# Ranks of the edge sort in three accumulators in turn, and three columns of eight scattered by GpSimd in place of four

## The chip, the cores and the metric

The kernel runs on one core of one Trainium2 chip. The metric is the device time of one execution in microseconds; the median of the runs counts. Engines are named as in the profile: PE (TensorE's matmuls), PEld (its weight loads), DVE (VectorE), ACT (ScalarE), POOL (GpSimd) and SP (SyncE).

## What is computed

Four graph layers follow each other on 6250 nodes of 256 features and 100000 edges; each ends with a residual sum and a layer norm. The layers gather a row for each edge's source and sum the rows by the edge's target:

```python
edge_index = jnp.stack([src, dst])
x = _layernorm(x + _L0_gnn_ref(x, edge_index, ...))                # conv with batch norms
x = _layernorm(x + _L1_gnn_ref(x, edge_index, edge_type_8, ...))   # 3 relational layers
x = _layernorm(x + _L2_gnn_ref(x, ..., src, dst, edge_type_16))    # messages and a GRU cell
x = _layernorm(x + _L3_gnn_ref(x, edge_index, ...))                # attention
```

The kernel doesn't trust the order of the edges. It first sorts them into buckets of 128 target nodes, padded to chunks of 128 edges (832 chunks). The change is in this sort alone.

## The kernel before

**Edges and groups.** The edges lie as 128 partitions by 784 columns. Eight columns are a group (NG = 8, 98 groups, t counts them), sixteen a block (SB = 16, 49 blocks, NSB; i counts them). The places of the edges of a column are found in four steps.

**Ranks (PE, L1134 to L1141).** For a group PE adds up, in one PSUM accumulator (bank 6, 392 columns: 49 buckets by 8 columns), how many edges of each bucket came before. `tri` counts the partitions ahead within the group, `trest` then adds the rest of the group, so that the accumulator stands at the group's end. Rank t waits on s_read for DVE's reading of group t-1, runs the `trest` matmul of group t-1 (L1139) and the `tri` matmul of group t (L1140), which increments s_rank.

**Slots (DVE, L1612 to L1632).** `rank_of` waits on s_rank, multiplies the ranks with the marks of the buckets (L1616, increments s_read) and reduces them (L1620). Once per block `slots_of` (L1624 to L1632) turns the sums into a chunk number, a partition and a row of the table slots_d, and increments s_slots.

**Placing.** A column of edges is placed in one of two ways. Of each eight columns POOL scatters the first POOL_G = 4 by an indirect DMA into slots_d (L703): column k of a group has a semaphore s_sc[k] of its own, and its scatter waits for the one of the group before on the same semaphore. The other four are routed by PE: DVE makes two one-hot marks of the column, over partitions (`ohp`, L1641) and over chunks (`ohc`, L1642); ACT scales the first by the two payload words (`lhs`, L774, two copies); PE multiplies them (L1149 into columns 0 to 511, L1151 into the other 320) and adds up in banks 0 to 3 over the whole sort. Marks and copies lie in a ring of ROUTES = 6; s_sort, incremented by each route, frees a place for DVE and ACT.

**Order.** DVE works two blocks ahead with ranks and slots (AHEAD_SB = 2): in each half of block i it makes the marks of the half and then reads the rank of the same half of block i+2. PE's program has the same order: rank, the routes of the half, rank, the routes of the other half, and then `gram(i)` (L1157, four matmuls on X, bank 7). All queues are in order. Before its first route PE sums X's rows in bank 5 (L1164), which ACT reads at L764 and L765, and ACT's copies of the routes stand behind these two. After the sort SP waits for all scatters and loads slots_d (L575), and DVE adds the routed words (L1681).

Of the kernel before, what the change touches and what calls it, by code (L numbers as in the profile page):

```python
# [22 lines left out]
ACT = mybir.ActivationFunctionType  # L23
# [3 lines left out]
N, D, E = 6250, 256, 100000  # L27
NT = -(-N // P)
# [5 lines left out]
NG = 8  # L34
NSB = -(-(EC + 1) // SB)
EP = NSB * SB
TB = EP // NG
POOL_G = (4, 4)
ROUTES = 6
AHEAD_SB = 2  # L40
TU = 7
TI = NT // TU
U = 16
# [35 lines left out]
READY0 = 4  # L79
assert 0 < ETAIL <= 32 and EC % NG >= max(POOL_G) and EC // NG == TB - 1  # L80
assert max(N, P << LOW_BITS) <= 30 * 1024 and LEAST % (1 << LOW_BITS) == 0
assert NT == TU * TI and NCH == U * CI and U == 2 * GR and NCH % GR == 0
assert all(U * min(t + READY, CI) * NT >= (t + 1) * NCH for t in range(NT)) and CI - READY <= NT
# [41 lines left out]
def program(nc, a, out):  # L125
    ctx = ExitStack()
    with ctx:
        def sb(name, shape, dt=F32):
            return ctx.enter_context(nc.sbuf_tensor(name, shape, dt))

        def sem(name):
            return ctx.enter_context(nc.semaphore(name))

        def dram(name, shape, dt=F32):
# [12 lines left out]
        X = sb("X", [P, NT, D])  # L147
# [7 lines left out]
        g = sb("g", [P, U, D + R2])  # L155
# [7 lines left out]
        ones = sb("ones", [P, P])  # L163
# [5 lines left out]
        ps = ctx.enter_context(nc.psum_tensor("ps", [P, 8, 512], F32))  # L169
# [3 lines left out]
        mine = AY[:, 0:m_words].bitcast(F16).rearrange("p (b e) -> p b e", e=EP)  # L173
# [13 lines left out]
        tri, trest, ones_h, col_h = (Y[:, y0 + k * (P // 2):y0 + (k + 1) * (P // 2)].bitcast(F16) for k in range(4))  # L187
# [20 lines left out]
        marked = gflat[:, 3 * EP:3 * EP + 2 * NG * NT].rearrange("p (s g b) -> p s g b", s=2, g=NG)  # L208
        base_b = gflat[:, 3 * EP + 2 * NG * NT:3 * EP + 3 * NG * NT]
# [98 lines left out]
        assert o3 <= NT * D  # L308
        own = [Y[:, scratch3 + b * TU * D:scratch3 + (b + 1) * TU * D] if b < TI - 2 else
               gflat[:, (b - TI + 2) * TU * D:(b - TI + 3) * TU * D] for b in range(TI)]  # L310
        own = [v.rearrange("p (t d) -> p t d", d=D) for v in own]
        assert scratch3 + (TI - 2) * TU * D <= NT * D

# [18 lines left out]
        def lhs(r, k):  # L332
            return spare[r // 2][:, r % 2, k, :]

        product_t = Y[:, y_prod:y_prod + KD * D].rearrange("p (k d) -> p k d", k=KD)
        b2_row, mu_row, cov, nmu_row = rows0[:, 2, :], rows0[:, 3, :], rows0[:, 4:6, :], rows0[0:1, 6, :]
# [15 lines left out]
        s_prep_act = sem("s_prep_act")  # L352
# [9 lines left out]
        s_wt = sem("s_wt")  # L362
        s_mine = sem("s_mine")
        s_rank = sem("s_rank")
        s_read = sem("s_read")
# [6 lines left out]
        s_blank_d = sem("s_blank_d")  # L372
        s_sc = [sem(f"s_sc{k}") for k in range(max(POOL_G))]
        s_loaded = sem("s_loaded")
# [111 lines left out]

        sort_cols = [NG * s + k for s in range(2) for k in range(POOL_G[s], NG)]
        per_sb, half_sb = len(sort_cols), (0, NG - POOL_G[0], len(sort_cols))
        out_uses = [(NT + 1) // 2, NT // 2]
# [8 lines left out]
        def bucket_by_size(engine, t):  # L498

            _, values = nc.values_load_multi_w_load_instructions(  # L500
                order_of[0:1, bass.ds(t, 1)], engines=(engine,), min_val=0, max_val=NT - 1,
                skip_runtime_bounds_check_because="the buckets' numbers in another order")
            return values[0]
# [28 lines left out]
        def batch(v, b):  # L532
            return v[:, TU * b:TU * (b + 1), :]

# [15 lines left out]
        def _(sp):  # L550
# [20 lines left out]

            for k in range(max(POOL_G)):
                sp.wait_ge(s_sc[k], 16 * NSB * sum(k < n for n in POOL_G))
            sp.wait_ge(s_read, TB)
# [168 lines left out]
        def _(act):  # L743
# [17 lines left out]
                     ps[:, k, :].rearrange("p (b k o) -> p k b o", b=KD, k=KD)).then_inc(s_wt, 1)  # L761

            act.wait_ge(s_prep_pe, PREP_PE["csum"])
            act.activation(mu_row, ps[:, 5, 0:D], ACT.Copy, scale=1.0 / N).then_inc(s_prep_act, 1)  # L764
            act.activation(nmu_row, ps[0:1, 5, 0:D], ACT.Copy, scale=-1.0).then_inc(s_prep_act, 1)  # L765

            for i in range(0, NSB):
                for q in range(per_sb):
                    at, n = sort_cols[q], per_sb * i + q
# [3 lines left out]
                    for k in range(WORDS):  # L773
                        ins = act.activation(lhs(r, k), ohp[:, r, :], ACT.Copy,  # L774
                                             scale=payload[:, bass.ds(SB * i + at, 1), k])
# [303 lines left out]
        def _(pe):  # L1079
# [7 lines left out]
            for w in range(4):  # L1087
                for b in range(KD):
                    for k in range(KD):
                        at = (b * KD + k) * P  # L1090
                        ins = pe.transpose(ps[:, w, at:at + P], nat0[:, w, b, k * P:(k + 1) * P], ident[:, :])
# [27 lines left out]
            def marks(t):  # L1119
                return mine[:, :, NG * t:NG * (t + 1)]  # L1120

            def over_groups(v):
                return v.rearrange("p (b g) -> p b g", g=NG)

            ranks = over_groups(ps[:, 6, 0:NT * NG])

            pe.wait_ge(s_const, 7)
            pe.wait_ge(s_mine, NT)
            for t in range(TB):
                ins = pe.matmul(over_groups(ps[:, 7, 0:NT * NG]), ones_h, marks(t), start=(t == 0), stop=(t == TB - 1))  # L1130
            ins.then_inc(s_prep_pe, 1)
            pe.wait_ge(s_prep_dve, PREP_DVE["base"])
            pe.matmul(ps[:, 6, 0:NT * NG], ones[0:1, :], base_b[0:1, :], start=True, stop=False, skip_group_check=True)

            def rank(t):

                if t:
                    pe.wait_ge(s_read, t)
                    pe.matmul(ranks, trest, marks(t - 1), start=False, stop=False, skip_group_check=True)  # L1139
                pe.matmul(ranks, tri, marks(t), start=False, stop=(t == TB - 1), skip_group_check=True)\  # L1140
                    .then_inc(s_rank, 1)  # L1141

            def route(n):

                r, last = n % ROUTES, n == per_sb * NSB - 1
                pe.wait_ge(s_ohc, n + 1)
                pe.wait_ge(s_lhs, ROUTES + n + 1)
                for k in range(WORDS):
                    pe.matmul(ps[:, 2 * k, :], lhs(r, k), ohc[:, r, 0:512], start=(n == 0), stop=last,  # L1149
                              skip_group_check=True)  # L1150
                    ins = pe.matmul(ps[:, 2 * k + 1, 0:NCH - 512], lhs(r, k), ohc[:, r, 512:NCH], start=(n == 0),  # L1151
                                    stop=last, skip_group_check=True)
                ins.then_inc(s_sort, 1)

            def gram(t):
                for k in range(KD):
                    pe.matmul(ps[:, 7, k * D:(k + 1) * D], X[:, t, k * P:(k + 1) * P], X[:, t, :],  # L1157
                              start=False, stop=False, skip_group_check=True)

            for t in range(2 * AHEAD_SB):  # L1160
                rank(t)
            pe.wait_ge(s_x_in, 32)
            for t in range(NT):
                ins = pe.matmul(ps[:, 5, 0:D], ones[:, :], X[:, t, :], start=(t == 0), stop=(t == NT - 1))  # L1164
            ins.then_inc(s_prep_pe, 1)
            pe.matmul(ps[:, 7, :], zrow[:, 0:P], zrow, start=True, stop=False, skip_group_check=True)
            pe.wait_ge(s_prep_act, PREP_ACT["nmu"])
            for i in range(NSB):
                for q in range(per_sb):
                    if i + AHEAD_SB < NSB and q in half_sb:  # L1170
                        rank(2 * (i + AHEAD_SB) + half_sb.index(q))
                    route(per_sb * i + q)
                gram(i)
            for k in range(KD):
                ins = pe.matmul(ps[:, 7, k * D:(k + 1) * D], nmu_row[:, k * P:(k + 1) * P], mu_row[0:1, :], start=False,
                                stop=True, skip_group_check=True)
# [8 lines left out]
            for o, lo, hi in ((ps[0:1, 6, :], 0, 512), (ps[0:1, 7, 0:NCH - 512], 512, NCH)):  # L1185
                pe.matmul(o, ones[0:NT, 0:1], count_m[:, 1, lo:hi], start=True, stop=False)
                ins = pe.matmul(o, minus_one[0:NT, :], count_m[:, 2, lo:hi], start=False, stop=True)
# [345 lines left out]
        def _(dve):  # L1533
# [74 lines left out]
                link(dve.tensor_tensor(bases[:, :, k + 1], bases[:, :, k], counts[:, :, k], ALU.add))  # L1608
            dve.sem_inc(s_prep_dve, 1)

            ranked = ps[:, 6, 0:NT * NG].rearrange("p (b g) -> p b g", g=NG)

            def rank_of(t, at, s):

                dve.wait_ge(s_rank, t + 1)
                ins = dve.tensor_tensor(marked[:, s].rearrange("p g b -> p b g"), ranked, mine[:, :, bass.ds(at, NG)],  # L1616
                                        ALU.mult)
                ins.then_inc(s_read, 1)
                dve.wait_ge(s_read, t + 1)
                link(dve.tensor_reduce(slot_f[:, NG * s:NG * (s + 1)], marked[:, s], AX, ALU.add))  # L1620
# [23 lines left out]

            for i in range(-AHEAD_SB, NSB):
                for s in range(2):
                    if i >= 0:
                        dve.wait_ge(s_slots, i + 1)
                        for q in range(half_sb[s], half_sb[s + 1]):
                            slot_marks(i, q)  # L1650
                    if i + AHEAD_SB < NSB:
                        rank_of(2 * (i + AHEAD_SB) + s, SB * (i + AHEAD_SB) + NG * s, s)
                if i + AHEAD_SB < NSB:
# [15 lines left out]
            for k in range(2):  # L1669
                ins = dve.tensor_scalar(count_m[:, 1 + k, :], count_m[:, 0, :], bound_c[:, k:k + 1], prow[0:NT, :],  # L1670
                                        ALU.is_ge, ALU.mult)
# [149 lines left out]
            for k in range(KD):  # L1821
                ins = dve.tensor_scalar(diagonals[:, KD + k, :], ident[:, :], cvec[:, k:k + 1], None, ALU.mult)
# [379 lines left out]
```

## Time and profile before

| what | us |
|---|---|
| median of 3 runs | 8975.67 (8972.37 to 9003.58) |
| the profiled execution | 8997.92 |
| its span, first to last instruction | 8996.0 |
| PE busy in the span | 6359.2 (71%) |
| POOL busy | 5138.8 (57%) |
| DVE busy | 4786.9 (53%) |
| ACT busy | 2385.3 (27%) |
| mean granted TensorE clock | 0.832 of full speed |

The profile is of one execution. Busy shares are means over stages of very different kind; the sort takes less than the first tenth of the span, all that follows gathers and sums rows. An idle time is put down to a releaser, "remote" and "another core or an unknown queue" being those for which the profile finds none. The ends of matmuls are modelled, their starts are measured.

### The profile page before, as it was taken

The page shows a single profiled execution, that of the slowest core. Times are in us where ns is not written, and L with a number is a line of the kernel's source. Part 1 is how long each engine was busy: PE and PEld are TensorE (multiplying, and loading weights), DVE is VectorE, ACT ScalarE, POOL GpSimd, SP SyncE. Part 2 cuts the span into 40 slices and gives each one's busy share as a digit, 9 for nine tenths or more (in the row PEclk, how much of TensorE's full clock was granted, in tenths as well). Part 3 has the DMA queues.
Part 4 walks back from the last instruction along what each step waited for, and adds up shares of the span by engine and source line. Part 5 has one row for each costly group of instructions (what it writes and reads, how often), then busy time and mean ns, then how long its engine had stood idle before and what let it go on. Part 6 is the DMA issues. An engine that isn't in the chain of part 4 may idle for free.

```text
span 8996.0 us, 103600 instructions
## 1 busy us (share of the span) xinstructions
PE 6359.2 (71%) x25277; PEld 4099.7 (46%) x25277; DVE 4786.9 (53%) x16507; ACT 2385.3 (27%) x7342; POOL 5138.8 (57%) x5401
## 2 busy tenths in 40 slices
PE   6665777779777777677776555555777776888881
PEld 3333555554345545444444334333444444656551
DVE  5555455545444444344343444444555556888788
ACT  2331111112111111011111222220222224666665
POOL 3555666650266666566665666665666655655550
PEclk8887787879888899788888776667998887999995
DMA  1002333333444445444445666664333335666662
GB/s 50 2 2 58 113 90 90 90 80 131 139 128 135 134 135 132 110 135 136 137 136 148 210 212 208 213 199 105 90 92 91 89 79 161 191 190 190 188 184 72
DMA packets 562307, 1141.83 MB, mean 127 GB/s; under 512 B 115031, under 2 KB 307516, under 8 KB 561598
## 3 DMA queue, kind: packets, MB, share of 16 engines
q0 software_dynamic: 252160, 659.72, 27.8%
q1 hardware_dynamic: 195886, 366.27, 11.7%
q10 hardware_dynamic: 113680, 109.21, 3.6%
q8 instruction: 228, 3.74, 0.2%
q14 instruction: 353, 2.89, 0.1%
HBM read 822.31 MB, written 312.46 MB: 126 GB/s over the span
## 4 chain that ended last, share of the span: by engine, by line
PE 40%; another core or an unknown queue 21%; DVE 15%; issue 15%; ACT 4%; DMA 1%; DVEq 1%; ACTq 1%; POOL 0%; SPq 0%; POOLq 0%
PE ps L1108 12%; PE ps L1324 6%; PE ps L1294 4%; DVE AY L1775 4%; PE ps L1512 3%; PE ps L1499 2%; PE ps L1490 1%; PE ps L1485 1%; PE ps L1456 1%; DVE oh L1758 1%; DVE rows L1758 1%; PE ps L1097 1%; DVE AY L2061 1%; PE ps L1457 1%
## 5 line engine op out<-in xcount | busy, mean ns | idle before, releaser
L1775 DVE TENSOR_TENSOR AY<-AY,ps 128x256 f32 (+1 forms) x4160 | 1735.6, 417 | 3183.6 <-remote 1671.9
L718 POOL DMA_INDIRECT g<-rel_d,edges x2496 | 2365.3, 948 | 1716.6 <-issue 667.7
L1108 PE MATMUL ps<-g,rows 128*128 128x256 f32 (+1 forms) x4160 | 1375.1, 453 | 282.5 <-DVE AY L1775 121.4
L1108 PE MATMUL ps<-g,oh 128*128 128x256 f32 (+1 forms) x4160 | 1381.6, 450 | 146.1 <-DVE oh L1758 54.7
L1108 PEld LDWEIGHTS ps<-g,rows 128*128 128x128 f32 x4160 | 866.4, 228 | 648.8 <-issue 396.8
L718 POOL DMA_INDIRECT g<-rows_d,edges x832 | 800.9, 963 | 504.2 <-issue 206.7
L1108 PEld LDWEIGHTS ps<-g,oh 128*128 128x128 f32 x4160 | 868.0, 227 | 406.8 <-issue 212.9
L718 POOL DMA_INDIRECT g<-in_x,edges x832 | 793.8, 954 | 448.8 <-issue 211.2
L1324 PE MATMUL ps<-AY,turned 128*128 128x512 f32 x1568 | 829.1, 656 | 202.7 <-ACT turned L745 114.6
L2048 DVE TENSOR_REDUCE AY<-ps 128x4 f32<-128x512 f32 x832 | 570.0, 685 | 202.8 <-PE ps L1490 128.3
L1758 DVE TENSOR_SCALAR oh<-col,edges 128x128 f32<-128x128 f32 x2080 | 617.0, 297 | 48.5 <-DMA marks_d<-oh 24.1
L1758 DVE TENSOR_SCALAR rows<-col,edges 128x128 f32<-128x128 f32 x2080 | 607.3, 292 | 51.3 <-issue 41.4
L745 ACT ACTIVATE wt<-ps 128x512 f32<-128x512 f32 (+1 forms) x448 | 250.0, 558 | 1410.6 <-remote 595.8
L703 POOL DMA_INDIRECT slots_d<-AY,g x392 | 381.1, 972 | 362.4 <-DVE g L1632 245.6
L738 POOL DMA_INDIRECT g<-att_d,edges x416 | 394.1, 947 | 330.3 <-PE ps L1512 174.4
L738 POOL DMA_INDIRECT AY<-att_d,edges x416 | 393.9, 947 | 272.1 <-PE ps L1512 175.5
L1324 PEld LDWEIGHTS ps<-AY,turned 128*128 128x128 f32 x1568 | 324.4, 211 | 468.2 <-issue 318.5
L745 ACT ACTIVATE turned<-ps 128x256 f32<-128x256 f32 (+1 forms) x343 | 141.4, 412 | 1150.7 <-remote 920.2
L745 ACT ACTIVATE AY<-ps 128x512 f32<-128x512 f32 (+3 forms) x421 | 179.1, 443 | 999.9 <-remote 674.2
L1023 ACT ACTIVATE g<-g 128x64 f32<-128x64 f32 x1664 | 419.2, 334 | 0.0
L1023 ACT ACTIVATE AY<-AY 128x64 f32<-128x64 f32 x1664 | 418.7, 334 | 0.0
L1097 PE MATMUL ps<-AY,turned 128*128 128x256 f32 x784 | 235.4, 427 | 199.5 <-DVE AY L1890 93.4
(378 smaller groups left out, 9566.2 us busy)
## 6 DMA issues: line engine op xcount, KB each, us to landing
rel_d<-wt ACTq DMA_DIRECT2D x392, 256.0 KB
turned_d<-AY SPq DMA_DIRECT2D x104, 512.0 KB
wt<-turned_d SPq DMA_DIRECT2D x104, 512.0 KB
AY<-marks_d SPq DMA_DIRECT2D x104, 512.0 KB
rel_d<-g SPq DMA_DIRECT2D x49, 1024.0 KB
g<-rel_d,edges POOLq DMA_INDIRECT x2496
marks_d<-oh SPq DMA_DIRECT2D x104, 256.0 KB
marks_d<-rows SPq DMA_DIRECT2D x104, 256.0 KB
```

The lines of the kernel that those rows point to most:

```text
L703: pool.indirect_dma_start(out=slots_d, out_offset=bass.IndirectOffsetOnAxis(ap=slot_row[:, at:at + 1], axis=0), in_=payload[:, at, :], in_ ...
L718: pool.indirect_dma_start(out=g[:, j, 0:width], out_offset=None, in_=table, in_offset=bass.IndirectOffsetOnAxis(ap=edges[:, word, c:c + 1] ...
L738: pool.indirect_dma_start(out=group_at(k)[:, j, 0:W4], out_offset=None, in_=att_d, in_offset=bass.IndirectOffsetOnAxis(ap=edges[:, 0, c:c ...
L745: return act.activation(o, v, ACT.Copy)
L1023: ins = act.activation(row[:, h * F:(h + 1) * F], row[:, h * F:(h + 1) * F], ACT.Copy, scale=row[:, D + h:D + h + 1])
L1097: ins = pe.matmul(o, turned[:, b, k * P:(k + 1) * P], w[:, k, :], start=(k == 0), stop=(k == KD - 1))
L1108: ins = pe.matmul(sum_slot(order, j), one_hot_at(j % OHS), g[:, j, 0:width], start=True, stop=True)
L1294: ins = pe.matmul(ps[:, q, :], turned[:, b, k * P:(k + 1) * P], relations[0][:, k, q * 512:(q + 1) * 512], start=(k == 0), stop=(k == KD - 1))
L1324: ins = pe.matmul(ps[:, 4 + q % 2, :], turned[:, 0, k * P:(k + 1) * P], w[:, k, q * 512:(q + 1) * 512], start=(k == 0), stop=(k == KD - 1))
L1758: dve.tensor_scalar(one_hot_at(j % OHS), col[:, :], edges_f[:, 2, k:k + 1], None, ALU.is_equal)\
L1775: dve.tensor_tensor(tile_at(A, t, width), tile_at(A, t, width), sum_slot(order, j), ALU.add)\
L2048: dve.tensor_reduce(red[:, c % 4, :], ps[:, SP_BANKS[c % len(SP_BANKS)], :].rearrange("p (h e) -> p h e", h=H), AX, ALU.max)\
```

## The change

Three things change. POOL scatters three columns of eight, with three semaphores, and PE routes the other five; a block has 10 routes in place of 8. The ranks are kept in three accumulators (banks 4, 5 and 6) in turn: group t uses bank 4 + t % 3, waits for DVE's reading of group t-3, adds the rest of group t-3, the whole of the groups t-2 and t-1 (`ones_h`), and its own `tri`. And PE issues ranks two groups further ahead (RANKS_ON = 2). The sum over X moves from bank 5 to bank 0, behind a wait for ACT's copies of the weights.

```diff
-POOL_G = (4, 4)
+POOL_G = (3,3)
 ROUTES = 6
 AHEAD_SB = 2
+RANKS, RANK_BANK, RANKS_ON = 3, 4, 2
...
-            act.activation(mu_row, ps[:, 5, 0:D], ACT.Copy, scale=1.0 / N).then_inc(s_prep_act, 1)
-            act.activation(nmu_row, ps[0:1, 5, 0:D], ACT.Copy, scale=-1.0).then_inc(s_prep_act, 1)
+            act.activation(mu_row, ps[:, 0, 0:D], ACT.Copy, scale=1.0 / N).then_inc(s_prep_act, 1)
+            act.activation(nmu_row, ps[0:1, 0, 0:D], ACT.Copy, scale=-1.0).then_inc(s_prep_act, 1)
...
-            ranks = over_groups(ps[:, 6, 0:NT * NG])
+            def ranks(t):
+                return over_groups(ps[:, RANK_BANK + t % RANKS, 0:NT * NG])
...
-            pe.matmul(ps[:, 6, 0:NT * NG], ones[0:1, :], base_b[0:1, :], start=True, stop=False, skip_group_check=True)
+            for t in range(RANKS):
+                pe.matmul(ps[:, RANK_BANK + t, 0:NT * NG], ones[0:1, :], base_b[0:1, :], start=True, stop=False,
+                          skip_group_check=True)
 
             def rank(t):
 
-                if t:
-                    pe.wait_ge(s_read, t)
-                    pe.matmul(ranks, trest, marks(t - 1), start=False, stop=False, skip_group_check=True)
-                pe.matmul(ranks, tri, marks(t), start=False, stop=(t == TB - 1), skip_group_check=True)\
+                if t >= RANKS:
+                    pe.wait_ge(s_read, t - RANKS + 1)
+                    pe.matmul(ranks(t), trest, marks(t - RANKS), start=False, stop=False, skip_group_check=True)
+                for u in range(max(t - RANKS + 1, 0), t):
+                    pe.matmul(ranks(t), ones_h, marks(u), start=False, stop=False, skip_group_check=True)
+                pe.matmul(ranks(t), tri, marks(t), start=False, stop=(t >= TB - RANKS), skip_group_check=True)\
                     .then_inc(s_rank, 1)
...
-            for t in range(2 * AHEAD_SB):
+            for t in range(2 * AHEAD_SB + RANKS_ON):
                 rank(t)
+            pe.wait_ge(s_wt, 4)
             pe.wait_ge(s_x_in, 32)
             for t in range(NT):
-                ins = pe.matmul(ps[:, 5, 0:D], ones[:, :], X[:, t, :], start=(t == 0), stop=(t == NT - 1))
+                ins = pe.matmul(ps[:, 0, 0:D], ones[:, :], X[:, t, :], start=(t == 0), stop=(t == NT - 1))
...
-                    if i + AHEAD_SB < NSB and q in half_sb:
-                        rank(2 * (i + AHEAD_SB) + half_sb.index(q))
+                    if q in half_sb and 2 * (i + AHEAD_SB) + half_sb.index(q) + RANKS_ON < TB:
+                        rank(2 * (i + AHEAD_SB) + half_sb.index(q) + RANKS_ON)
                     route(per_sb * i + q)
...
-            ranked = ps[:, 6, 0:NT * NG].rearrange("p (b g) -> p b g", g=NG)
+            def ranked(t):
+                return ps[:, RANK_BANK + t % RANKS, 0:NT * NG].rearrange("p (b g) -> p b g", g=NG)
...
-                ins = dve.tensor_tensor(marked[:, s].rearrange("p g b -> p b g"), ranked, mine[:, :, bass.ds(at, NG)],
+                ins = dve.tensor_tensor(marked[:, s].rearrange("p g b -> p b g"), ranked(t), mine[:, :, bass.ds(at, NG)],
                                         ALU.mult)
```

## Rows read from the trace of the kernel before

**Rows 1.** The page, section 5: costliest groups of the whole span.

```profile
L1775 DVE TENSOR_TENSOR AY<-AY,ps 128x256 f32 (+1 forms) x4160 | 1735.6, 417 | 3183.6 <-remote 1671.9
```

**Rows 2.** Windows: stage, its length, busy us and instructions by engine, clock, DMA.

```profile
91.00:748.00 657.00, 415.76 (x1925) 210.36 (x1924) 380.67 (x1236) 239.96 (x772) 366.18 (x377) 0.82 0.02 2
...
775.00:8996.00 8221.00, 5877.28 (x23088) 3848.79 (x23088) 4341.43 (x15125) 2131.03 (x6549) 4747.38 (x4992) 0.83 0.47 137
```

**Rows 3.** The chain of waits, 91 to 748 us: start, length, what.

```profile
by line: another core or an unknown queue 31.2%; issue 14.7%; DVE edges L1642 10.8%; PE ps L1149 8.2%; DVE g L1616 8.0%; DVE edges L1641 7.7%; PE ps L1151 5.7%; DVE g L1620 5.0%; ACT oh L774 1.8%; PE ps L1157 1.5%; ACT turned L774 1.2%; ACT
...
319.00 12.13 another core or an unknown queue
...
502.10 7.04 another core or an unknown queue
```

**Rows 4.** Table of waits in the sort: us in total, times, longest.

```profile
DVE g L1616 <- remote: 201.8, 34, 12.7
...
DVE edges L1641 <- remote: 23.7, 6, 7.2
```

**Rows 5.** Timeline around a wait of DVE: start, length, engine, line, [idle before].

```profile
307.90 0.17 DVE L1632 SCALAR_TENSOR_TENSOR g<-g 128x16 int32<-128x16 f32 x1
...
316.30 0.18 DVE L1632 SCALAR_TENSOR_TENSOR g<-g 128x16 int32<-128x16 f32 x1
...
316.50 0.33 PE L1139 MATMUL ps<-AY 128*128 128x392 f16 x1
316.67 0.33 PE L1140 MATMUL ps<-AY 128*128 128x392 f16 x1
...
320.21 0.30 PE L1151 MATMUL ps<-edges,oh 128*128 128x320 f16 x1
...
331.16 0.82 DVE L1616 TENSOR_TENSOR g<-ps,AY 128x392 f32<-128x392 f32 x1 [12.16 <-remote]
...
332.03 0.51 PE L1139 MATMUL ps<-AY 128*128 128x392 f16 x1 [11.53 <-DVE g L1616]
```

**Rows 6.** Timeline of POOL: firsts of two runs of scatters, the last before a pause.

```profile
308.35 1.09 POOL L703 DMA_INDIRECT slots_d<-AY,g  x1 [1.80 <-DVE g L1632]
...
327.43 0.96 POOL L703 DMA_INDIRECT slots_d<-AY,g  x1 [0.30 <-issue]
...
499.54 1.08 POOL L703 DMA_INDIRECT slots_d<-AY,g  x1 [1.32 <-issue]
```

**Rows 7.** The table slots_d: scatters and the load back, durations, first and last start.

```profile
L703 POOL DMA_INDIRECT slots_d<-AY,g x392: 952/958/1179, 64.2 to 746.5; - x196
...
L575 SPq DMA_DIRECT2D AY<-slots_d x1: 352/352/352, 748.7 to 748.7; - x1
```

**Rows 8.** Timeline of DVE without waits: marks, ranks and slots.

```profile
332.61 0.26 DVE L1641 TENSOR_SCALAR edges<-AY,g 128x128 f16<-128x128 f16 x1
...
333.12 0.25 DVE L1641 TENSOR_SCALAR edges<-AY,g 128x128 f16<-128x128 f16 x1
...
334.64 0.81 DVE L1616 TENSOR_TENSOR g<-ps,AY 128x392 f32<-128x392 f32 x1
...
336.09 0.17 DVE L1624 CAST g<-g 128x16 int32<-128x16 f32 x1
...
336.90 0.25 DVE L1641 TENSOR_SCALAR edges<-AY,g 128x128 f16<-128x128 f16 x1
```

**Rows 9.** Timeline of PE: gram, two routing matmuls in a dense stretch, one after a gap.

```profile
305.63 1.03 PE L1157 MATMUL ps<-X 128*128 128x256 f32 x4
...
310.54 0.38 PE L1149 MATMUL ps<-edges,rows 128*128 128x512 f16 x1
...
310.89 0.38 PE L1149 MATMUL ps<-edges,rows 128*128 128x512 f16 x1
...
755.33 0.64 PE L1149 MATMUL ps<-edges,turned 128*128 128x512 f16 x1
```

**Rows 10.** Groups of instructions by line, 91 to 748 us: the scatters.

```profile
L703 POOL DMA_INDIRECT slots_d<-AY,g x376 | 365.6, 972 | 297.5 <-DVE g L1632 185.3 <-issue 112.2
```

## The prediction

> **What bounds the kernel now.** I read the windows by stage first: the change touches only the sort, and [rows 2] show that its routed part runs from 91 to 748 us, 657 us for 49 blocks of 16 columns, 13.4 us each. The reader is to see that no engine is full there: PE is busy 416 us, DVE 381, Pool 366, ACT 240, the DMA engines 2%. The costliest line of the page [rows 1] belongs to the graph layers that follow, 8221 us which the edit doesn't touch, so whatever the sort gains or loses passes to the end: the first gather waits for the sorted edges.
>
> Then I read the chain of waits of the same stretch [rows 3]. 31.2% of it, 205 us, lies at no engine but at "an unknown queue", in a few long pieces (12.1 us at 319.0, 7.0 us at 502.1). The table of waits says whose they are [rows 4]: DVE sat 201.8 us before L1616, the reading of the ranks, 34 times, longest 12.7. The timeline takes one apart [rows 5]: PE ran the second rank matmul L1140 at 316.67, DVE ended its last mark at 319.0, PE its last routing matmul at 320.5. Then PE, ACT and DVE stand still until L1616 starts at 331.16. That instruction waits for one thing, the increment of s_rank that L1140 carries, 14 us old by then. PE's next rank matmul starts at 332.03, as soon as the read has ended. So the increment was late, not the work.
>
> What was active meanwhile is Pool. It scatters 16 columns on end from 308.35 to 328.4, one per 1.26 us [rows 5, 6], and DVE comes free 2.8 us after that. The onset fits as well. After a pause of Pool of 1.80 us (308.35) the stall starts 10.7 us into the scatters, in the second block of the run; the first block went through in 8.4 us (DVE's L1632 at 307.90 and 316.30 [rows 5]). After a pause of 1.32 us (499.54 [rows 6]) it starts at 502.1, only 2.6 us in. I read this so: while Pool issues scatters without a break, semaphore increments of PE come late, and a pause of about two microseconds clears them. Now a block costs Pool 8 x 1.26 = 10.1 us and DVE only some 8.3, so Pool never pauses until the stall itself makes it. That is a reading of coincidences, and the forecast hangs on it.
>
> **The change, part by part.**
>
> Pool scatters 3 of 8 columns. 6 x 1.26 = 7.6 us per block in place of 10.1 [rows 6]. With three semaphores in place of four a scatter now waits for the one three before it, issued 3.8 us earlier. The last scatter is issued at 746.5 and SP, which waits for all of them to land, issues the reading back at 748.7 [rows 7]: landing takes at most 2.2 us, so this costs nothing. If it took the 5.05 us that four scatters last, the upper bound that the pitch leaves, Pool would be back at 10.1.
>
> DVE makes 10 pairs of marks in place of 8. A pair takes 0.51 us (332.61 to 333.12), a rank 1.45 (334.64 to 336.09, multiply and reduce), the slots 0.81 (336.09 to 336.90) [rows 8]. Before: 8 x 0.51 + 2 x 1.45 + 0.81 = 7.8, measured 8.4 in the block without a stall, so 0.6 for collisions. After: 8.8, with the same collisions 9.4 us.
>
> PE routes 10 in place of 8: each four matmuls, two pitches of 0.35 (310.54 to 310.89), so 7.0 us. Its ranks take four matmuls per group, not two (one more matmul for each of the two groups between): 8 per block, which follow each other at 0.17 (316.50, 316.67 [rows 5]), 1.4 us. The four matmuls of L1157 take 1.03. Together 9.4 us at 2.4 GHz, against 7.3 before [rows 9]. PE and DVE are then level and both above Pool's 7.6.
>
> ACT makes 20 scaled copies at 0.32 (an estimate from 240 us busy over 49 x 16 copies, 0.31 each [rows 2]): 6.3 us, under both.
>
> Ranks two groups ahead in three accumulators. In place of the group that DVE reads next, PE has issued two more by then: a late s_rank increment may be late by a block before DVE notices. At the same time PE's wait on s_read is for a read three groups back. Behind rank's wait stand all routing matmuls of the half block, and ACT and DVE wait for those through the ring of six; with the wait gone early this costs nothing. The bank moved to 0 for the column sum waits for four copies that ACT did long before 60 us, nothing. Two accumulators more to start: two short matmuls, under 2 us, hidden before 91 us, where all wait for X's sums.
>
> So a block takes 9.4 us at best. At that pace Pool works 7.6 and pauses 1.8 us or more, the pause after which [rows 6] show a whole block without a stall, and if it is too short, the stall lengthens it. To the 9.4 I add 0.6 us for two engines that are both nearly full and hand over through six slots. 10.0 us per block: 49 x (13.4 - 10.0) = 167 us less.
>
> Bounds: below, DVE without collisions, 8.8 us, -225 us. Above, every wait stays, and the added DVE work comes on top, +49 x 1.0.
>
> One rule speaks against the change. The row: 376 scatters took 365.6 us, 0.97 each, beside 0.96 of an undisturbed one in the timeline [rows 6, 10], so DVE's marks cost Pool about 0.01 us per scatter. The Trainium skill (SBUF — State Buffer, the shared port pair) says that a VectorE tensor_scalar in a two-port mode blocks GpSimd from writing descriptors for its whole length. By the row Pool needs 7.6 us; by the rule up to 7.6 plus the marks' length. The trace doesn't bear it out at that size.
>
> **Rivals.**
> - Ring of six. Late increments are those of the routes (s_sort) too, and DVE and ACT wait for a route six back, only about half a block. For: DVE already waits 23.7 us at L1641 for an unknown releaser [rows 4]. Against: in a block after a pause it doesn't. If half the 205 us stays: 10.0 + 2.1 = 12.1 us per block, -64 us, 8912.
> - No change in sum: the stalls keep their length because another block's worth of work meets them. 13.4 per block, 8976.
> - The other side: the lateness follows PE's own traffic of matmuls and increments, not Pool's scatters. Before the stall PE had been running its matmuls densely and at the short duration of 2.4 GHz, which speaks for it; that they end 2.8 us after Pool's last scatter speaks against it. Then the 205 us stay and each block pays DVE's extra 1.0: +50 us, 9026. It decides if stalls are seen with Pool idle.
> - Clock. A routing matmul of 512 columns takes 0.64 us after a gap of PE, 0.38 in a dense stretch [rows 9]; all at 1.2 GHz a block's 9.4 us double to 18.8, +265 us, 9241. Against it: PE would be nearly always busy. The Trainium skill (TensorE: Matmul & The Clock Gate, Part 1) says the throttled state is the default and activity releases it; the trace agrees, the mean granted clock being 0.82 in the routed part.
> - Pool locked out, the rule above worked out from rows: 10 x (0.25 + 0.43) = 6.8 us of marks [rows 8] on top of 7.6 makes 14.4 us per block, +49 us, 9025.
>
> **How the numbers follow.** The sum is made against the profiled execution, 8997.92 us with a span of 8996.0: 8831. It is 22 us above the median 8975.67, so I forecast 8809. Chances: forecast (9.4 to 11.5 us per block, 8780 to 8883) 0.70; ring of six 0.12; no change 0.07; PE's own traffic 0.07; clock 0.03; Pool locked out 0.01. Faster by over 0.5% (45 us, about what this kernel's runs can tell from no change) 0.82, same 0.07, slower 0.11. The likeliest's own range is 8780 to 8883; reaching down for less than full collisions and up over the ring of six gives 8765 to 8935, which leaves out some 0.18.
>
> **What would show it.** Right: the routed part is 490 us long; Pool scatters in runs of 6 with a pause of 2 us or more; DVE's wait before L1616's successor falls from 202 us to under 20; granted clock above 0.95 there; everything after the sort keeps its length. Wrong: long waits on "an unknown queue" that moved to the marks or to ACT's copies (ring of six); waits that start with Pool idle (PE's traffic); a granted clock near 0.5; scatters longer than 1.1 us. What would break the sum is above all that the link between Pool's unbroken scatters and the late increments is only a coincidence.

## The result, and the profile after

The changed kernel takes 8766.01 us (median of 4 runs, 8756.10 to 8773.54), the kernel before 8979.73 beside it: ratio 0.976, 95% interval 0.9743 to 0.9776. That is 214 us less. The direction and what bound the kernel were forecast; the size was not: 167 us and a range down to 8765 were forecast, and the ratio puts the changed kernel at 8760 on the scale of the median shown before, just under the range.

The routed part of the sort by windows (stage, length, busy us and instructions of PE, PEld, DVE, ACT, POOL, then the granted clock, the DMA share and GB/s):

```profile
91.00:539.00 448.00, 445.62 (x2471) 246.98 (x2470) 433.20 (x1418) 294.78 (x956) 277.22 (x284) 1.00 0.03 3
```

It ends at 539 us where it ended at 748 [rows 2]. DVE is busy 97% of it and PE by its modelled ends 99%; the clock is granted in full, 0.82 before. The table of waits of this stretch, longest first:

```profile
POOL slots_d L704 <- DVE g L1640: 106.7, 47, 14.7
POOL slots_d L704 <- issue: 72.6, 233, 1.8
ACT turned L775 <- DVE edges L1649: 50.9, 32, 2.1
ACT oh L775 <- DVE edges L1649: 49.6, 31, 2.0
ACT rows L775 <- DVE edges L1649: 47.8, 30, 2.1
PEld ps L1155 <- issue: 32.1, 123, 0.3
DVE edges L1649 <- PE ps L1157: 19.2, 2, 16.8
```

The wait of 201.8 us before the reading of the ranks (L1616 in [rows 4], now L1624) has no row any more. ACT waits for DVE's marks and Pool for its slots, 47 times, 2 us each but for the start. The chain of waits has "an unknown queue" no longer among its first twelve parts, where it was 31.2% [rows 3]:

```profile
by line: DVE edges L1650 31.9%; DVE edges L1649 19.5%; DVE g L1624 15.1%; DVE g L1628 11.6%; issue 8.7%; PE ps L1155 2.4%; DVE g L1632 1.8%; DVE g L1633 1.8%; PE ps L1157 1.8%; DVE g L1636 1.4%; DVE g L1638 0.9%; DVE g L1634 0.8%; DVEq L164
```

The timeline of Pool and DVE through one block (start, length, [idle before]), beside [rows 5, 6 and 8]:

```profile
304.50 0.17 DVE L1640 SCALAR_TENSOR_TENSOR g<-g 128x16 int32<-128x16 f32 x1
...
304.96 1.09 POOL L704 DMA_INDIRECT slots_d<-AY,g  x1 [1.98 <-DVE g L1640]
...
305.13 0.25 DVE L1649 TENSOR_SCALAR edges<-AY,g 128x128 f16<-128x128 f16 x1
...
305.64 0.40 DVE L1649 TENSOR_SCALAR edges<-AY,g 128x128 f16<-128x128 f16 x1
...
306.85 0.64 DVE L1650 TENSOR_SCALAR edges<-edges,g 128x832 f16<-128x832 f16 x1
...
307.41 0.81 DVE L1624 TENSOR_TENSOR g<-ps,AY 128x392 f32<-128x392 f32 x1
...
311.40 0.96 POOL L704 DMA_INDIRECT slots_d<-AY,g  x1 [0.31 <-issue]
...
313.88 0.17 DVE L1640 SCALAR_TENSOR_TENSOR g<-g 128x16 int32<-128x16 f32 x1
...
314.33 1.09 POOL L704 DMA_INDIRECT slots_d<-AY,g  x1 [1.97 <-DVE g L1640]
```

Slots at 304.50 and at 313.88: a block takes 9.38 us, again and again. Pool scatters six columns in 7.4 us and pauses 1.97. A mark takes 0.25 us; the one at 305.64, begun 0.7 us after the start of a scatter, takes 0.40. The first gather of the layers, which is what the rest waits for, starts 206 us earlier (774.37 in the trace before):

```profile
568.48 0.99 POOL L719 DMA_INDIRECT g<-in_x,edges  x1 [24.19 <-DVE edges L1694]
```

From there to the end it is 8201 us against 8222. In nine other runs whose layers are the same this rest took 8182 to 8216, so I take these 20 us for spread of the layers and not for the sort; no run shows it, and 8222 is the longest of all.

### The profile page after: what moved, and what is told of

Its sections match the earlier page's. It is cut to its first block, busy times and chain, and to the rows that moved or that the text cites. A ratio compares the mean times of both kernels' runs of the same rounds, so it can differ in the third digit from the quotient of the medians.

```text
span 8769.9 us, 105363 instructions
## 1 busy us (share of the span) xinstructions
PE 6380.8 (73%) x25864; PEld 4099.8 (47%) x25864; DVE 4844.9 (55%) x16703; ACT 2445.7 (28%) x7538; POOL 5049.1 (58%) x5303
## 4 chain that ended last, share of the span: by engine, by line
PE 40%; another core or an unknown queue 21%; DVE 16%; issue 14%; ACT 4%; DMA 1%; DVEq 1%; ACTq 1%; SPq 0%; POOL 0%; POOLq 0%
PE ps L1109 11%; PE ps L1331 6%; PE ps L1301 4%; PE ps L1519 4%; DVE AY L1783 3%; PE ps L1463 2%; PE ps L1506 2%; DVE edges L1650 2%; PE ps L1497 2%; PE ps L1492 2%; PE ps L1464 1%; PE ps L1098 1%; DVE AY L2069 1%; DVE edges L1649 1%
## 5 line engine op out<-in xcount | busy, mean ns | idle before, releaser
L1783 DVE TENSOR_TENSOR AY<-AY,ps 128x256 f32 (+1 forms) x4160 | 1744.1, 419 | 3173.0 <-remote 1681.1
L1109 PE MATMUL ps<-g,rows 128*128 128x256 f32 (+1 forms) x4160 | 1327.6, 440 | 278.7 <-DVE AY L1783 113.0
L1109 PEld LDWEIGHTS ps<-g,rows 128*128 128x128 f32 x4160 | 835.4, 220 | 636.0 <-issue 381.6
L704 POOL DMA_INDIRECT slots_d<-AY,g x294 | 287.9, 979 | 246.2 <-DVE g L1640 169.3
```

The source lines that it names most:

```text
L1109: ins = pe.matmul(sum_slot(order, j), one_hot_at(j % OHS), g[:, j, 0:width], start=True, stop=True)
L1783: dve.tensor_tensor(tile_at(A, t, width), tile_at(A, t, width), sum_slot(order, j), ALU.add)\
```

## The experiments

**Each half of the change alone.** The first kernel is the changed one with `POOL_G = (4, 4)`: only the accumulators and the ranks ahead are left. The second is the kernel before with three of eight scattered.

```diff
-POOL_G = (3,3)
+POOL_G = (4, 4)
```

> The changed kernel with four of eight columns scattered again, so that only the three accumulators and the ranks issued ahead are left of the change. If unbroken scatters of Pool delay the increments (my theory), Pool needs 10.1 us per block and never pauses by itself, the waits move from the ranks to the ring of six (marks L1649, copies L775), and a block takes 11.5 to 13.4 us: 0 to -95 us against before. If the ranks ahead are what removed the stalls (rival), a block takes Pool's 10.1 us: -160 us or more.

Measured: ratio to before 1.0003 (0.9992 to 1.0014). No gain at all. The waits have moved, as a view of waits in the sort shows:

```profile
DVE edges L1649 <- remote: 198.9, 40, 8.4
```

and the timeline of a stall (start, length, [idle before]):

```profile
301.78 0.17 DVE L1640 SCALAR_TENSOR_TENSOR g<-g 128x16 int32<-128x16 f32 x1
...
308.16 0.25 DVE L1649 TENSOR_SCALAR edges<-AY,g 128x128 f16<-128x128 f16 x1 [4.22 <-remote]
...
312.97 0.96 POOL L704 DMA_INDIRECT slots_d<-AY,g  x1 [0.30 <-issue]
...
315.22 0.26 DVE L1649 TENSOR_SCALAR edges<-AY,g 128x128 f16<-128x128 f16 x1 [5.14 <-remote]
...
320.31 0.17 DVE L1640 SCALAR_TENSOR_TENSOR g<-g 128x16 int32<-128x16 f32 x1
```

The ranks are there in time; now it is the marks that wait for an old route's s_sort. 201.8 us before L1616 became 198.9 before L1649. Making one consumer deaf to late increments handed the wait to the next.

> The kernel before with three of eight columns scattered and nothing else: ranks in one accumulator, each waiting for the reading before. My theory: Pool works 7.6 us per block and pauses, so the 12 us stalls are gone; late increments in the last third of a run of scatters can cost the second rank of a block a microsecond or so; 9.4 to 11 us per block, -120 to -200 us. Rival (the ranks ahead removed the stalls): the stalls stay, and DVE's two extra pairs come on top, 13.4 to 14.4 us per block, 0 to +50 us.

```diff
-POOL_G = (4, 4)
+POOL_G = (3, 3)
```

Measured: 8766.10 us, ratio 0.9749 (0.9726 to 0.9771). The whole gain, with the ranks in one accumulator. The wait before the ranks, 201.8 us before, in its table of waits:

```profile
DVE g L1616 <- remote: 1.8, 1, 1.8
```

**Is it Pool's scatters, and is it their being unbroken?** Two edits of the kernel before, both with four of eight columns. In the first Pool does something else than scatter after each eighth scatter:

```diff
 ROUTES = 6
+PAUSES = 6
...
                         in_=payload[:, at, :], in_offset=None).then_inc(s_sc[k], 16)
+                if t % 2:
+                    for _ in range(PAUSES):
+                        paused += 1
+                        pool.memset(gflat[:, 4016:4352], 0.0).then_inc(s_pause, 1)
+                        pool.wait_ge(s_pause, paused)
```

> The kernel before, four of eight scattered, with six small chained memsets of Pool after every eighth scatter: Pool gets some 2.5 us more work per block in which it scatters nothing. My theory: the long waits before L1616 (202 us) nearly vanish, and a block takes what Pool now needs, 12.1 to 12.8 us: -30 to -65 us, although Pool has more to do. Rival, the lateness follows PE's own traffic or Pool's being busy with anything: the waits stay and the time is the same or higher, up to +120 us.

Measured: 8926.03 us, ratio 0.9934 (0.9915 to 0.9953), some 56 us faster with more to do for the very engine that was the suspect. Pool's timeline and DVE's row in the table of waits:

```profile
314.29 0.96 POOL L706 DMA_INDIRECT slots_d<-AY,g  x1 [0.31 <-issue]
315.25 3.10 POOL L712 MEMSET g<- 128x336 f32 x6
318.62 0.96 POOL L706 DMA_INDIRECT slots_d<-AY,g  x1 [0.28 <-POOL g L712]
```

```profile
DVE g L1624 <- remote: 52.1, 22, 3.4
```

The six memsets take 3.1 us together, a block therefore 13 us of Pool, and Pool is busy without a gap: 475 of 612 us by the windows, and what is left is the 0.30 us between its instructions. Yet DVE's wait falls from 201.8 to 52.1 us and the longest from 12.7 to 3.4. So it isn't Pool's being busy that holds the increments up, it is scattering without a break.

> The kernel before without any scatter (left out: the columns that Pool places, so half the edges are missing from the output; every other engine does the same work). My theory: no wait for an unknown releaser before L1616, blocks of 8.3 us, DVE's own work, the routed part 410 us: -240 to -260 us. Rival, PE's own traffic of matmuls and increments: the 12 us waits stay, and the time is within 20 us of before.

```diff
             for k in range(max(POOL_G)):
-                sp.wait_ge(s_sc[k], 16 * NSB * sum(k < n for n in POOL_G))
+                pass
...
-                for k in range(POOL_G[t % 2]):
+                for k in range(0):
```

Measured: 8693.71 us, ratio 0.967 (0.9649 to 0.969), 288 us less. Two slots rows of its timeline, and its window:

```profile
306.50 0.18 DVE L1632 SCALAR_TENSOR_TENSOR g<-g 128x16 int32<-128x16 f32 x1
...
314.30 0.17 DVE L1632 SCALAR_TENSOR_TENSOR g<-g 128x16 int32<-128x16 f32 x1
```

```profile
91.00:453.00 362.00, 346.94 (x1861) 189.78 (x1859) 352.13 (x1206) 227.75 (x746) 0.00 (x0) 1.00 0.00 1
```

7.8 us per block and no wait for the unknown. PE sends its increments more densely than in the kernel before, and none is late: PE's own traffic is out as a cause. And 7.8 is exactly the sum of DVE's instructions in [rows 8], so the 0.6 us of collisions that I added belongs to the scatters, not to DVE.

**Late increment or held-up DVE?** The views name the releaser of these waits "remote", and by them alone DVE itself could have been held up. The kept traces also record single increments with their times, though not all of them (81 of the 98 of s_rank in the kernel before), and these show that DVE starts as soon as the increment is recorded. The increment of [rows 5], from the matmul of 316.67, is recorded at 331.13, 0.03 us before L1616 starts. Four of s_sort stand behind it, at 331.19, 331.25, 331.31 and 331.37, for routes that PE had ended by 320.5. Over the routed part the recorded increments of s_rank come up to 14.3 us after the end of their matmul, while those that DVE and ACT make come within 0.02 us. In e4 those of s_rank do so too.

In the changed kernel PE's increments are late still, s_rank's by up to 3.5 us: one comes at 304.12, 1.1 us after a run's last scatter has ended, and five of s_sort follow it in 0.3 us. But DVE reads that rank at 311.73, and nobody waits. In e2 s_rank's come up to 2.8 us late, which cost the 1.8 us above.

**How long a run, or how much load?** The kernel of e2 with the same work per block, in runs of twelve:

```diff
-                if t % 2 == 0:
-                    pool.wait_ge(s_slots, t // 2 + 1)
+                if t % 4 == 0:
+                    pool.wait_ge(s_slots, min(t // 2 + 2, NSB))
```

> As e2_pool_only (three of eight scattered, one accumulator), but Pool waits for the slots of two blocks and then scatters both: the same work per block, 7.6 us, in runs of 12 scatters (15.2 us) with a pause of 3.6 us, in place of runs of 6 with 1.8 us. My theory (the length of an unbroken run counts): from some 10 us into each run the increments are late, DVE waits until the run has ended, 11 to 13.5 us per block, +80 to +200 us against e2_pool_only. Rival (Pool's mean load counts): as e2_pool_only within 10 us.

Measured: 8926.24 us, ratio 0.9933 (0.991 to 0.9955), against 8766 with runs of six: 160 us for the same scatters. The table of waits of DVE, and the window:

```profile
DVE g L1616 <- remote: 75.0, 20, 6.7
DVE edges L1641 <- PE ps L1151: 45.8, 26, 3.7
DVE edges L1641 <- remote: 29.4, 12, 5.0
```

```profile
91.00:688.00 597.00, 472.64 (x2250) 242.59 (x2247) 424.78 (x1399) 290.38 (x934) 273.91 (x283) 0.86 0.02 2
```

Mean load doesn't explain it: Pool is busy 274 us of the stretch here and 278 in e2. Two prices add up. DVE waits 104 us for the unknown, and after such a gap PE's clock falls: granted 0.86 in this stretch, 1.00 in e2's, and another 45.8 us of DVE's waits are for routes that PE hadn't done yet, for which e2's table has no row. Together that is 150 us, and the stretch is 150 us longer than e2's 447. One part of my expectation doesn't hold: the waits don't all last until a run has ended. In the block I looked at DVE's L1616 starts at 321.36 after a wait of 2.88 us, with the run's last scatter still to come.

**Seven scatters.**

```diff
-POOL_G = (3,3)
+POOL_G = (3, 4)
```

> The changed kernel with three columns scattered of the first group of a block and four of the second: seven scatters, 8.8 us of Pool per block, nine routes. DVE then needs 8.9 us per block, PE 8.7, so Pool's pause would be 0.1 to 0.5 us. My theory: that isn't enough, increments come late again, the stalls return in part, a block takes 10 to 12.5 us, +30 to +150 us against the changed kernel. Rival (any drop of Pool's load below DVE's is enough): 8.9 to 9.0 us per block, -20 to -25 us against the changed kernel, the best so far.

> The kernel before with (3, 4) in place of (4, 4) and nothing else: ranks in one accumulator. My theory: as e5_three_four or worse, since DVE meets the late s_rank increments first: 10 to 13 us per block, 8800 to 8950 us. If the ranks ahead are worth something with a short pause, e5 is faster than this one by 20 us or more; if not, both are the same.

Measured: e5 8935.33 us, ratio 0.9944 (0.9926 to 0.9962); e7 8923.92 us, ratio 0.9931 (0.9914 to 0.9947). By the ratios both lose some 155 to 165 of the 214 us again, e5 by 15 us more than the upper end that I gave. With seven Pool has 8.8 us of work for a block of DVE that takes 9.1 without a stall. In e5's timeline the run that begins at 313.20 is followed at 322.62 by the next with no pause but the 0.30 us between any two scatters, fourteen on end; the pause of 6.69 us then comes out of a stall:

```profile
313.20 1.09 POOL L704 DMA_INDIRECT slots_d<-AY,g  x1 [9.22 <-DVE g L1640]
...
317.44 1.08 POOL L704 DMA_INDIRECT slots_d<-AY,g  x1 [0.62 <-DMA slots_d<-AY,g]
...
322.62 0.96 POOL L704 DMA_INDIRECT slots_d<-AY,g  x1 [0.30 <-issue]
...
337.97 1.09 POOL L704 DMA_INDIRECT slots_d<-AY,g  x1 [6.69 <-DVE g L1640]
```

One column in sixteen is the difference between none and nearly all of the stalls. The intervals of e5 and e7 overlap: the accumulators bring no gain that these runs can tell, at eight, six or seven scatters per block.

**The changed kernel and e2 on one chip, and five scatters.**

> The changed kernel once more, beside e2's on the same chip. 8766 us on a chip where before takes 8980, ratio 0.976.

> The kernel of e2_pool_only once more, on the same chip as e10. My theory: with Pool pausing, DVE sets the pace and the three accumulators are worth nothing: the same as e10 within 0.1%, 9 us. Rival: the six matmul groups more per block that PE is spared (8.7 against 9.4 us) show, up to 15 us faster than e10; or the ranks ahead are worth something, up to 15 us slower.

> As e11, with two columns scattered of the first group and three of the second: five scatters, 6.3 us of Pool, 11 routes. DVE, which sets the pace, gets another pair of 0.5 us: 9.9 us per block, +25 us against e11. If Pool's pauses of 2 us were still costing something, it would be less than that, or a gain.

Measured: e10 8760.09 us (0.9758, 0.9745 to 0.9772), e11 8766.11 us (0.9764, 0.975 to 0.9777), e12 8781.61 us (0.9778, 0.9763 to 0.9793). e10 and e11 can't be told apart. e12 is 16 us above e11, where I had put 25. The 0.5 us of another pair is there: its slots rows stand 9.86 us apart (303.58 and 313.44), e11's 9.40 (304.99 and 314.39), and its first gather starts 20 us later. The other 4 us lie in the layers. Of five, six, seven and eight scatters six is the best: with seven the stalls come back, with five DVE pays for another pair.

**Carried over to the layers.** The changed kernel, whose Pool asks for its gather buffers six or four chunks at a time:

```diff
-                    if c % SUM_GROUP[order] == 0 and summed(order, c - U):
-                        pool.wait_ge(s_mm, summed(order, c - U))
+                    last = min(c + RUN, NCH) - 1
+                    if c % RUN == 0 and summed(order, last - U):
+                        pool.wait_ge(s_mm, summed(order, last - U))
```

> The changed kernel, and in the first five gather passes of the layers Pool asks for its buffers six chunks at a time, not two: same gathers, but in runs of at most six with a wait between runs where the buffers were full. If the finding of the sort carries over, unbroken runs of Pool are behind part of the 1681 us that DVE waits for an unknown releaser at L1783, and pauses clear them: -30 to -200 us against the changed kernel. Rival (those waits have another cause, or the layers' Pool pauses often enough already): within 20 us; and the shorter lead of the gathers can cost something, up to +100 us.

> The same with runs of four. Theory: shorter runs, as much gain or more than by six, -30 to -200 us. Rival: as for six, with less lead lost, within 20 us.

Measured, on a chip where the kernel before takes 9033.25 us: 8910.40 us for six, ratio 0.9869 (0.9849 to 0.9889), and 9037.40 us for four, ratio 1.0005 (0.9995 to 1.0015). The changed kernel has 0.976 on other chips, so runs of six cost about 1.1% and runs of four 2.5%. DVE's wait for an unknown releaser, 1681.1 us of the whole span in the changed kernel's page (1750.0 in e10), rose in the tables of waits of e8 and of e9:

```profile
DVE AY L1785 <- remote: 1925.0, 405, 15.1
...
DVE AY L1785 <- remote: 2055.3, 399, 12.5
```

Both forecasts missed. Whether the late increments play a part in the layers stays open: grouping the waits also let Pool start again with up to 6 buffers free at once, with less lead, and the two weren't separated.

## Why the prediction was off

- **What bound the kernel: right.** The 202 us of [rows 4] were late increments, tied to Pool's unbroken scatters. The recorded increments show the first half of that sentence; e4 (no scatters, no waits), e3 (Pool busier, waits a quarter) and e6 (same load, longer runs, 160 us lost) show the second from three sides.
- **Pool's term: right.** 7.6 us of work per block, six scatters, pause 1.97 us. Landing costs next to nothing: 1.0 us of waits for it in the whole sort. But "at most 2.2 us" was read from the last scatter alone: in e5 the one at 317.44 had to wait for the landing of the one at 313.20 on the same semaphore, 4.2 us, more than the 3.8 that I counted on.
- **DVE's term: right.** 9.4 us was worked out and 9.38 measured. PE's 9.4 fits too, but e2, where PE has 8.7 us of work, has the same blocks: DVE sets the pace, and PE's term isn't tested apart from it.
- **The hand-over allowance: the step that failed.** To the 9.4 us I added 0.6 "for two engines that are both nearly full and hand over through six slots", an estimate from no row. It measured nothing: the blocks take 9.38 us, and 9.44 in the mean of the 46 between the third slots row and the last. Over these 46 blocks the difference to 10.0 is 26 us of the 39 by which the forecast of 167 fell short of the 206 that the first gather gained. With six places between them the block time is that of DVE's queue, even at 97% and 99% busy. The routed part took 448 us where I had put 490.
- **A second term mis-sized: the pace before.** I divided the routed part evenly, 657 us by 49, and took 13.4 us per block. But two of the 49 slots rows lie before 91 us, and after the last one DVE has marks alone to make. From the third slots row to the last, 46 blocks, the pace was 13.9 us before (97.50 to 736.86) and 9.44 after (95.77 to 530.09). That is 205 us: 46 x (13.9 - 10.0) is 179 where I had 167, 13 us more, and the 26 of the allowance make it 205. The ends nearly cancel: the third slots row comes 2 us earlier, the reading back follows the last one after 9.1 us in place of 11.8 ([rows 7] and the last row below), and the first gather follows the reading back 4 us later than before. The slots rows of before and of after:

```profile
97.50 0.17 DVE L1632 SCALAR_TENSOR_TENSOR g<-g 128x16 int32<-128x16 f32 x1
...
736.86 0.18 DVE L1632 SCALAR_TENSOR_TENSOR g<-g 128x16 int32<-128x16 f32 x1
```

```profile
95.77 0.17 DVE L1640 SCALAR_TENSOR_TENSOR g<-g 128x16 int32<-128x16 f32 x1
...
530.09 0.18 DVE L1640 SCALAR_TENSOR_TENSOR g<-g 128x16 int32<-128x16 f32 x1
```

The reading back after, from the view of slots_d:

```profile
L576 SPq DMA_DIRECT2D AY<-slots_d x1: 347/347/347, 539.2 to 539.2; - x1
```

- **The ranks ahead: no gain.** The sum had no term for them, but I counted on them as a cushion ("may be late by a block before DVE notices"). At four, at three and at three-and-four columns nothing shows of it (e1, e10 against e11, e5 against e7). The ring-of-six rival that I weighed at 0.12 is what happens where Pool doesn't pause: e1 is that rival with its full 199 us.
- **The range.** Its lower end, 8765, allowed for DVE with fewer collisions, and the pace of 13.9 wasn't in it. Had the sum stopped at 9.4 us it would have given 8780, and over 46 blocks from 13.9 to 9.4 some 8769, where the runs lie.
- **Pool locked out.** Scatters took 0.98 us each (277 us for 284 instructions) against 0.97 before, so Pool isn't held up. It is the other way round: a mark begun 0.5 to 0.7 us into a scatter takes 0.40 us in place of 0.25, one of L1650 0.64 in place of 0.43, and a block of DVE takes 8.4 us with scatters (the fast block of [rows 5]) and 7.8 without (e4). The Trainium skill (SBUF — State Buffer, the shared port pair) says that whichever of a two-port VectorE operation and a GpSimd operation starts first makes the other wait; the trace agrees in that DVE's instructions get longer beside a scatter that began first, but by 0.15 to 0.2 us, not by what is left of a scatter of 0.96; in which mode the marks run no view tells.

Still open: by which path scatters delay the increments, and, since the ends of matmuls are modelled, whether the matmul's real end or only its increment comes late. All variants here stop the issue of scatters and the transfers themselves together, so the runs don't tell the two apart.

## What to carry to other kernels

A long idle time before an instruction whose only wait was satisfied microseconds ago by the trace points at a late semaphore increment: look at what runs unbroken meanwhile, and at when it stops. Here an engine that had slack by its busy share, Pool with 56%, set the pace by having no pause, and taking a quarter of its work away and giving it to fuller engines paid 214 us. Here two engines were level with six buffers between them, and the block time was DVE's own sum, without an allowance. A pace is better read from two rows of the same line far apart than from a stretch divided by its blocks. And before making a consumer tolerant to lateness, check who is the next in line.

## What was unexpected of the hardware

- Increments of PE, and of PE alone among PE, DVE and ACT, come up to some 14 us late while GpSimd issues indirect DMAs one per 1.26 us without a break; a pause of 1.97 us after six of them keeps them harmless (still up to 3.5 us late), seven without a pause behind them don't, and twelve on end cost 160 us with the same work per block.
- Work on GpSimd can serve as the pause: with 3.1 us of memsets after eight scatters the waits fall from 201.8 to 52.1 us. Whether idling as long would do more wasn't run.
- Such stalls cost a second time through TensorE's clock: the mean granted clock is 0.82 in the routed part before, 0.86 in e6 and 1.00 wherever the stalls are gone (after, e2, e4). The Trainium skill (TensorE: Matmul & The Clock Gate, Part 1) calls the throttled state the default that activity releases; the trace agrees.
